# First attention stage: sixteen 512 KB weight loads, one per unit, in place of two 4 MB loads; the DMA queue's units written out

## What is computed

```python
# first attention (x: 2 x 1024 x 256, after layer norm)
q = rope(x @ Wq)              # 32 heads x 8
k = rope(x @ Wk)              #  8 heads x 8
v = x @ Wv                    #  8 heads x 8
scores = einsum('bkgtd,bksd->bkgts', q, k) / sqrt(8)     # causal mask
ctx = einsum('bkgts,bksd->bkgtd', softmax(scores), v)
x = x + ctx @ Wo + b_out
# first feed-forward: 4 experts, top 1
h = silu(x @ Wg[e]) * (x @ Wu[e])        # Wg, Wu: 4 x 256 x 1024
x = x + top_w * (h @ Wd[e])              # Wd: 4 x 1024 x 256
...
# later: keyed sum, the same four experts again, linear attention, eight experts top 2,
# a second attention (16 query heads, 4 key/value heads of width 16), eight experts top 2
```

## Time and profile before

| what | value |
|---|---|
| median of 3 runs | 2004.8 us (2002.64 to 2005.82) |
| profiled execution: its own time | 2006.96 us |
| profiled execution: span | 2005.2 us (1.76 us lie outside) |
| busy share of the span | PE 90%, DVE 56%, ACT 38%, POOL 28% |
| mean granted TensorE clock | 0.935 of full speed |
| chain that ended last | PE 70%, DVE 16%, issue 4%, DMA 3% |
| first attention, its units | about 98 us to 535 us of the span |

### The profile page before, as it was taken

How to read it: one execution, slowest core, us unless ns; L and a number is a source line. 1 busy time by engine, 2 the same in 40 slices (tenths; PEclk the granted TensorE clock), 3 DMA queues, 4 the chain that set the end, 5 groups by cost and what they waited for, 6 DMA issues and landing times.

```text
span 2005.2 us, 31961 instructions
## 1 busy us (share of the span) xinstructions
PE 1801.9 (90%) x10672; PEld 1012.1 (50%) x10673; DVE 1121.3 (56%) x2299; ACT 755.6 (38%) x1469; POOL 555.1 (28%) x954
## 2 busy tenths in 40 slices
PE   7799999999969999676999969888987999988888
PEld 4344444443346665354666636566553444455654
DVE  6688888887242221765222255733465888746334
ACT  3277777777421111112112111222132676752220
POOL 2322222222111111452111140266133222223650
PEclk9699999999689999778999989899996999998999
DMA  3311111113310000301000050122414122002223
GB/s 107 87 36 42 42 42 42 40 37 144 117 52 26 21 24 19 97 1 50 23 21 24 21 176 10 61 87 87 123 52 86 23 42 40 3 18 70 90 76 124
DMA packets 82074, 114.36 MB, mean 57 GB/s; under 512 B 17273, under 2 KB 61465, under 8 KB 81177
## 3 DMA queue, kind: packets, MB, share of 16 engines
q1 hardware_dynamic: 70808, 82.23, 14.4%
q0 software_dynamic: 11136, 30.42, 4.8%
HBM read 78.35 MB, written 33.69 MB: 56 GB/s over the span
## 4 chain that ended last, share of the span: by engine, by line
PE 70%; DVE 16%; issue 4%; DMA 3%; another core or an unknown queue 2%; POOL 1%; ACT 1%; SPq 0%; POOLq 0%; DVEq 0%; ACTq 0%
PE psum L1542 13%; PE psum L1064 9%; PE psum L1048 7%; DVE region_a L812 7%; PE psum L1563 7%; PE psum L1009 6%; PE psum L1781 4%; PE psum L1752 3%; PE psum L1763 2%; PE psum L1800 2%; PE psum L1552 2%; PE psum L1801 1%; PE psum L938 1%; PE psum L1033 1%
## 5 line engine op out<-in xcount | busy, mean ns | idle before, releaser
L812 DVE TENSOR_REDUCE region_a<-psum 128x1 f32<-128x640 f32 (+7 forms) x576 | 528.4, 954 | 109.1 <-PE psum L1014 57.6
L916 ACT ACTIVATE region_w<-psum 128x512 f32<-128x512 f32 x864 | 465.6, 600 | 222.7 <-PE psum L1048 219.3
L1542 PE MATMUL psum<-region_w,region_a 128*128 x608 | 271.2, 599 | 1.5 <-DVE region_a L1623 1.2
L1064 PE MATMUL psum<-region_w,region_a 128*32 128x512 f32 (+3 forms) x2304 | 253.8, 514 | 1.0 <-POOL region_w L739 0.6
L739 POOL TENSOR_SCALAR_AFFINE_SELECT region_w<-region_w 128x512 f32<-128x512 f32 x192 | 122.3, 637 | 458.7 <-ACT region_w L916 454.6
L1009 PE MATMUL psum<-region_a,y_norm 48*128 48x512 bf16 (+7 forms) x816 | 224.1, 351 | 4.9 <-DVE region_a L812 3.8
L1048 PE MATMUL psum<-y_norm,region_a 51*128 51x512 bf16 (+1 forms) x612 | 205.4, 399 | 7.0 <-DMA y_norm<-region_a 5.2
L1542 PEld LDWEIGHTS psum<-region_w,region_a 128*128 128x128 f32 x608 | 114.0, 193 | 132.2 <-issue 132.2
L1630 DVE TENSOR_TENSOR region_a<-psum,region_a 128x512 f32<-128x512 f32 x76 | 52.6, 692 | 215.1 <-PE psum L1542 215.1
L1430 POOL DMA_INDIRECT region_a<-token_rows,region_a x116 | 113.1, 975 | 147.5 <-DVE region_a L1406 86.8
L1563 PE MATMUL psum<-region_w,region_a 128*128 x608 | 137.7, 379 | 1.9 <-ACT region_a L1602 1.9
(11 more groups left out here) (220 smaller groups left out, 2692.7 us busy)
## 6 DMA issues: line engine op xcount, KB each, us to landing
y_norm<-a_q SPq DMA_DIRECT2D x132, 64.0 KB
token_rows<-y_norm SPq DMA_DIRECT2D x16, 512.0 KB, 5.2
y_norm<-answer_rows SPq DMA_DIRECT2D x16, 512.0 KB, 6.1
y_norm<-b_q SPq DMA_DIRECT2D x36, 128.0 KB
region_w<-in_f_wg SPq DMA_DIRECT2D x1, 4096.0 KB, 13.4
region_w<-in_f_wu SPq DMA_DIRECT2D x1, 4096.0 KB, 13.4
region_w<-in_f_wd SPq DMA_DIRECT2D x1, 4096.0 KB, 14.8
region_w<-answer_rows SPq DMA_DIRECT2D x8, 512.0 KB, 8.6
```

What stands on the lines that cost most here:

```text
L812: dve.tensor_reduce(dst, src, AX_X, ALU.max, negate=True).then_inc(self.ring_done.sem, 1)
L916: act.activation(self.p[col % P_RING][:, :, i % 4, :], c.bank[ST_BANKS[s % 3]].rearrange("p (h t) -> p h t", h=GQ), ACT.Exp, scale=self.sc ...
L1064: mm = pe.matmul(c.bank[ACC_BANK][32 * h:32 * h + 32, P * lo:512], self.vp[slot][:, j, :], self.p[col % P_RING][:, h, lo:4, :], start=(j = ...
L1542: mm = pe.matmul(bank[:, :], self.yt[:, f, :], w[:, f, bass.ds(own * self.hidden + 512 * half, 512)], start=(f == 0), stop=(f == FT - 1))
```

## The change

The gate and up weights are no longer two DMAs of 4 MB. `early_loads` makes sixteen DMAs of 512 KB (128 partitions x 1024 columns): two tensors, four column blocks, two halves of the 256 rows. They are now all of `side_loads`; the zero rows become a separate `first_load` behind unit 0. SP's units are all written out, in the first and in the second attention, so each of the 16 units of the first attention takes one piece from the list, behind its own loads. The down weights stay as they were. The experts' stages wait for 17 DMAs instead of 3.

```diff
-            if isinstance(u, int) and self.side_loads:
+            if u == 0 and self.first_load:
+                self.first_load(sp)
+            if self.side_loads:
                 self.side_loads.pop(0)(sp)
 
-        self.every_unit(sp, unit, ahead=2)
+        for u in range(self.units):
+            unit(u, u % SLOTS, self.units - 1 - u)
+        assert not self.side_loads
...
 class Weights(Stage):
+    PIECES = 4
...
-    def loads(self):
-        wg, wu, wd = self.dram
-        return [lambda sp, dst=dst, src=src: sp.dma_start(dst, src).then_inc(self.loaded, 16)
-                for dst, src in ((self.wg, wg.rearrange("(f p) n -> p f n", p=P)),
-                                 (self.wu, wu.rearrange("(f p) n -> p f n", p=P)),
-                                 (self.wd, wd.rearrange("(j p) n -> p j n", p=P)))]
+    def load(self, dst, src):
+        return lambda sp: sp.dma_start(dst, src).then_inc(self.loaded, 16)
+
+    def early_loads(self):
+
+        n = self.hidden // self.PIECES
+        return [self.load(dst[:, f, n * i:n * i + n], src[P * f:P * f + P, n * i:n * i + n])
+                for dst, src in ((self.wg, self.dram[0]), (self.wu, self.dram[1]))
+                for i in range(self.PIECES) for f in range(FT)]
+
+    def late_loads(self):
+        return [self.load(self.wd, self.dram[2].rearrange("(j p) n -> p j n", p=P))]
 
     def wait(self, eng):
-        eng.wait_ge(self.loaded, 16 * 3)
+        eng.wait_ge(self.loaded, 16 * (2 * FT * self.PIECES + 1))
...
-            attention("a0", 8, "a0_w", "a0_wo", "a0", "a0_bias", "a0_bo", [start.zero_rows] + w0.loads()[0:2], w0.loads()[2:3])
+            attention("a0", 8, "a0_w", "a0_wo", "a0", "a0_bias", "a0_bo", w0.early_loads(), w0.late_loads(), start.zero_rows)
```

More of the change, by code:

```diff
@@ L436, with __init__ @@
 class Attention(Stage):
-    def __init__(self, c, name, ln, hd, w, wo, tables, bias, bias_out, mask_q, identb, side_loads, late_loads):
+    def __init__(self, c, name, ln, hd, w, wo, tables, bias, bias_out, mask_q, identb, side_loads, late_loads, first_load):
         self.c, self.ln, self.hd = c, ln, hd
@@ L450, in __init__ @@
         self.scale = float(hd) ** -0.5
-        self.side_loads, self.late_loads = side_loads, late_loads
+        self.side_loads, self.late_loads, self.first_load = side_loads, late_loads, first_load
         self.dram = dict(w=w, wo=wo, tables=tables, bias=bias, bias_out=bias_out, mq=mask_q, identb=identb)
@@ L2292, in __init__ @@
         self.loaded = c.sem(name + "_loaded")
-    def sync(self, sp):
-        for load in self.loads():
-            load(sp)
-    def loads(self):
-        wg, wu, wd = self.dram
-        return [lambda sp, dst=dst, src=src: sp.dma_start(dst, src).then_inc(self.loaded, 16)
-                for dst, src in ((self.wg, wg.rearrange("(f p) n -> p f n", p=P)),
-                                 (self.wu, wu.rearrange("(f p) n -> p f n", p=P)),
-                                 (self.wd, wd.rearrange("(j p) n -> p j n", p=P)))]
+    def load(self, dst, src):
[7 more added lines that the diff above has]
+        return [self.load(self.wd, self.dram[2].rearrange("(j p) n -> p j n", p=P))]
     def wait(self, eng):
-        eng.wait_ge(self.loaded, 16 * 3)
+        eng.wait_ge(self.loaded, 16 * (2 * FT * self.PIECES + 1))
 class SharedWeights(Stage):
@@ L2407, in project, with attention @@
             last[0] = p
-        def attention(name, hd, w, wo, tables, bias, bias_out, side_loads=(), late_loads=()):
+        def attention(name, hd, w, wo, tables, bias, bias_out, side_loads=(), late_loads=(), first_load=None):
             ln = begin(name)
             a = Attention(c, name, ln, hd, t[w], t[wo], (t[tables + "_cos"], t[tables + "_sin"]), t[bias], t[bias_out],
-                          t["mask_q"], t["identb"], side_loads, late_loads)
+                          t["mask_q"], t["identb"], side_loads, late_loads, first_load)
             stages.append(a)
```

## The result

The changed kernel takes 1986.81 us (median of 4 runs, 1985.87 to 1988.84) where the kernel before takes 2003.72 beside it (4 runs). The ratio is 0.9907 with a 95% interval of 0.9893 to 0.9920, that is 16 to 21 us less. Faster was forecast, and the mechanism is the forecast one, but the size was forecast too small: 15.0 us. Taken by the ratio from the 2004.8 us of the first three runs, the time is 1986.2 us. Both times lie just under 1987, the low end of the range.

What follows compares the result with a forecast made beforehand. Small row-maxima copies behind 4 MB loads were taken to stall units 14 and 15 and cost the clock. -3.0 - 13.3 + 1.3 = -15.0 us gave 1989.8 us against the median of 2004.8; range 1987 to 1992, up to 2000 with rival A.

Steps and rivals of the forecast that it cites:

- Where the loss was, and its cause: Units 14 and 15 of the first attention: small half 1 copies wait in SP's queue behind 4 MB gate and up loads.
- the copy of 2.63 us at 73.64: The same 12 KB copy earlier in the kernel, taken as the example of one having the queue to itself.
- Unit 14, -3.03 us: First attention's unit 14 gets its steady 26.62 us; idle time and the slow clock behind it go, -3.03 us.
- Unit 15, -13.3 us: First attention's last unit takes 24.7 for 38.02 us: -13.3 us, 3.02 of it idle time and 10.3 the clock.
- the model of 24.7 us: Unit 15 without its stall: the second attention's last unit, 24.29 us, plus a 0.41 us wait for POOL.
- The projection, +1.3 us given back: Projection behind the first attention: clock dips as in the second, 9.68 us instead of 8.36; +1.3 us, bounds 0 and +1.3.
- The pieces cost nothing: Sixteen 512 KB loads, one in each unit, land in some 3.5 us, ahead of half 1; no cost.
- The written-out loop costs and gives nothing: SP's loop written out in both attentions: SP is not on the steady unit's chain, so no gain or loss.
- Rival A: The clock falls in unit 15 without the stall too: unit 15 35.0 us, time 1998.8 us; chance 0.24, wholly or in part.
- Rival B: Pieces make half 1 late in every unit, 3.03 us each: slower, about 2044 us; chance 0.05.

Runs made afterwards that it cites:

- experiment 2: Kernel before with SP's loop kept and two 4 MB loads issued behind half 1 of the row maxima of units 14 and 15; ratio 0.9932.
- experiment 4: Changed kernel with the two 4 MB loads whole behind units 3 and 7, nothing else loaded in the units; ratio 0.9948 to the kernel before.
- experiment 5: Changed kernel with seven up-weight pieces (3.5 MB) together behind unit 14, the other nine pieces behind units 1 to 9; ratio 0.999 to the kernel before.
- the kernel before again: The kernel before, unchanged, run and profiled again for scatter between executions; ratio 1.0008.
- the 14 score products: Up weights whole behind unit 14, gate weights in pieces, plus 14 extra score products ahead of PE's wait in unit 15; ratio 0.9964 to the kernel before.
- the change again: The changed kernel, unaltered, run and profiled again for scatter between executions; ratio 0.9918 to the kernel before.
- experiment 6: The changed kernel and the kernel before, each run again for scatter between executions; ratios 0.9918 and 1.0008 to the kernel before.
- experiment 1: Changed kernel with SP's units written out, but gate and up weights as two 4 MB loads behind units 13 and 14; ratio 1.0002 to the kernel before.
- experiment 3: Changed kernel with one load whole, the other in eight pieces: gate whole behind unit 13, 0.9935; up whole behind unit 14, 0.9976 to the kernel before.
- experiment 7: Up load whole behind unit 14, extra PE products ahead of unit 15's wait: 14 score products, 0.9964; four full float32 products, 0.9917 to the kernel before.

## Why the prediction was right or wrong

- *Where the loss was, and its cause:* right. Both 7 us DMAs left the chain, and experiment 2 shows by itself that the place in the queue was the cause. One reading behind it was wrong: the copy of 2.63 us at 73.64 did not have the queue to itself, SP had issued loads of q and k up to 73.19, just ahead of it. So a copy behind small loads is quick too; it is the 4 MB ahead of it that made the late ones late.
- *Unit 14, -3.03 us:* right for the profile it came from (29.65 to 26.62). The second profile of before lost only 1.61 us there, because its clock stayed up.
- *Unit 15, -13.3 us:* too small; measured 38.02 - 23.66 = -14.36. The step that was mis-sized is the model of 24.7 us, taken from the second attention's last unit (24.29 us) plus 0.41; it is too long by 1.04. From the first score to score 10 (0.2 us behind the row at 499.16) the unit takes 6.4 us here and 6.1 there, although it has the 0.41 us wait for POOL and the second attention's has not; so most of that wait was hidden and should not have been added in full. From score 10 on it takes 17.3 us here and 18.15 there. The rows of that part differ mainly in two places, by 0.60 and 0.27 us: the second attention's order turns two finished halves of outputs there (L1033), the first's only one (L1037), with the other ahead of score 10; and the last value product waits longer for POOL. In the second attention, kernel before, then in the first, kernel after:

```profile
1763.84 0.60 PE L1033 MATMUL psum<-identf,region_a 128*128 128x128 f32 x4
1766.51 0.60 PE L1033 MATMUL psum<-identf,region_a 128*128 128x128 f32 x4
1775.04 0.43 PE L1064 MATMUL psum<-region_w,region_a 128*32 128x128 f32 x8 [0.60 <-POOL region_w L739]
...
496.38 0.66 PE L1037 MATMUL psum<-identf,region_a 128*128 128x128 f32 x4
506.11 0.66 PE L1037 MATMUL psum<-identf,region_a 128*128 128x128 f32 x4
516.17 0.42 PE L1068 MATMUL psum<-region_w,region_a 128*32 128x128 f32 x8 [0.33 <-POOL region_w L743]
```

That these differences are the cause is read from the rows; no run tests it. In the prediction's own split the idle time, 3.02 us, was right, and the clock's part is 11.3 us (14.36 less 3.02), not 10.3.

- *The projection, +1.3 us given back:* wrong, and the larger miss. It took 8.37 us (527.01 - 518.64), clock 1.00, in both profiles of the change; nothing was given back. From the copy at the end of unit 15 to the products L394 are 4.02 us in eight of twelve profiles, and 5.57 to 6.12 in the four others (experiments 4, 5, the kernel before again, and the 14 score products). Of the six profiles whose clock was up through unit 15, only that of experiment 4 shows such a fall. Even the second attention's projection, the example, took 8.37 us instead of 9.7 in two of the twelve (the change again and the kernel before again). So such a fall exists, but I made one stage's example the expectation; it should have been an end of the range.
- *These two terms are the whole miss inside the stage:* -15.0 becomes -3.03 - 14.36 = -17.4 us, and from the first steady pair of maxima (138.07 before, 137.46 after) to L394 (538.69, 520.68) the two profiles differ by 17.4 us. Against the median of before that gives 1987.4 us, still inside the range; the last 0.6 us down to the measured 1986.81 are less than the runs scatter. In the first pair of profiles another 0.6 us came ahead of the units and 2.5 behind; whether the change has a part in the 2.5, experiment 6 leaves open.
- *The pieces cost nothing:* right. 3.6 to 3.7 us to landing against 3.5 taken, and every steady unit at 26.62.
- *The written-out loop costs and gives nothing:* right (experiment 1).
- *Rival A, the clock falls anyway:* it did not come, in two profiles of the change and three of experiments 2, 3 and 4 whose last unit has no late half. Its evidence was sound, though: once the half was late the clock fell in this unit in six of seven profiles, and experiment 7 shows it falling with only 0.21 us of idle time.
- *Rival B, late in every unit:* it did not come, and its price of 3.03 us a unit lies between two cases: 1.9 us with the clock kept, 5.7 without (experiment 4).

## What to carry to other kernels

A small DMA that an engine waits for should not be issued close behind a large one on the same queue: here 12 KB took 6.9 us instead of 2.6. Either cut the large load so that each piece has landed before the next small one, or move it behind the last small one; both gave the same stage time here. And price a stall by what it does to the clock as well: 3 us of waiting cost 14 us where the clock did not come back, and gaps of about 2 us cost 1.6 to 5.7 us where it held or came back within the unit. And a stage taken as the model of another is one example: where the two differ, the difference belongs in the sum, and what only sometimes happens there belongs in the range.

## What was not expected of the hardware

- PE busy for 28.29 of 28.30 us at 0.50, and 27.40 of 27.40 at a mean of 0.51 in experiment 3, did not raise the clock; in units that also make maxima it came back after about 3.5 us or 9 us (experiment 4).
- Filling a 3 us wait with 14 products of 51 rows (3.18 us busy) did not keep the clock in the profiled execution; four float32 products of 128 x 128 x 512 (3.70 us) did. By the Trainium skill (TensorE: Matmul & The Clock Gate, section "What's actually happening") the gate follows how busy PE has been. The trace with the 14 products does not agree as far as busy time in the profile goes: 3.18 us busy and 0.21 idle, and the clock fell to 0.50.
- Two gaps of about the same length (2.10 and 1.88 us) in the same execution: one kept the clock, the other lost it (experiment 4).
